# Four-layer graph network: attention masks in pairs, rings in pairs, elu as a maximum

## The chip, the cores and the metric

The kernel runs on one core of a Trainium2 chip. The metric is the device time of one execution in microseconds (us); the median of several runs is given. TensorE multiplies matrices, VectorE and ScalarE work elementwise, GpSimd does small preparation and issues some DMAs, and SyncE issues the others. Each engine works through its own queue in order and waits on semaphores for the others.

## The reference, cut to what matters

Four layers, each with a layer norm, a relu, a graph layer and a residual. The first layer is two graph attentions with 8 heads of 32; the last is one with 4 heads of 64. N is 2500 nodes, E is 40000 edges.

```python
def gat_conv(x, W, al, ar, b, src, dst):          # layer 0, twice
    h = (x @ W).reshape(N, H, D)
    el = jnp.einsum('nhd,hd->nh', h, al)
    er = jnp.einsum('nhd,hd->nh', h, ar)
    e = jax.nn.leaky_relu(el[src] + er[dst], NEG_SLOPE)
    m = jax.ops.segment_max(e, dst, num_segments=N)
    ex = jnp.exp(e - m[dst])
    s = jax.ops.segment_sum(ex, dst, num_segments=N)
    alpha = ex / s[dst]
    out = jax.ops.segment_sum(alpha[:, :, None] * h[src], dst, num_segments=N)
    out = out.reshape(N, H * D) + b
    return jax.nn.elu(out)
...
e = jnp.exp(-jax.nn.leaky_relu(s, ALPHA))          # last layer, each of 4 heads
rowsum = jax.ops.segment_sum(e, src, num_segments=n_nodes)
hp = jax.ops.segment_sum(e[:, None] * h[dst], src, num_segments=n_nodes)
hp = hp / rowsum[:, None]
return jax.nn.elu(hp)                              # and elu again over all heads
```

## The kernel before, in words

The edges are turned once into a dense matrix of counts C, 20 source tiles of 128 rows by 2560 target columns in fp16. `exp(leaky_relu(a + b))` is a product of two exponentials on either side of a + b = 0, so an attention head is a matrix product over masks: where the sum is positive one pair of factors holds, elsewhere the other. The scaled features stand in UV (high and low half in fp16), and TensorE multiplies them by the masked counts.

`attention` runs three times: twice with 8 heads (`split` False) and once with 4 (`split` True). The stage in question is its second half, the loop over heads. A head is cut by target columns into PARTS parts (2 of 1280 columns, or 4 of 640). One part of one head is called a unit here; every attention has 16 units, each over NT = 20 source tiles.

For each tile of a unit:

- ScalarE writes `Rm`, a relu of the target row terms (`rows`, broadcast by a DMA from SyncE, two buffers) with the tile's bias `cB`, scaled so that it is zero or huge (L1109).
- VectorE makes the mask `M` as the minimum of `Rm` and the counts (L1153). With `split` False some tiles are done on VectorE alone in one scalar_tensor_tensor from `rows` (L1156): the last of each four, less the two in MORE_ON_ACT, so 8 of a head's 40.
- In the last attention VectorE also makes `Mn` = C - M, the rest of the counts, for the 12 tiles of a unit that are not in TURNED (L1143). For the 8 in TURNED, TensorE takes five more matmuls with the counts themselves and negated features VS (L1243). With `split` False that is done for every tile (L1248).
- TensorE runs 10 regions (L1240), 132 or 130 columns wide, into four PSUM banks. Two sets of four banks alternate between units.

The rings: `Rm`, `M` and `Mn` have SG slots (4, in the last attention 5). VectorE waits for TensorE to have finished the tile SG before (s_P). ScalarE waits before relu s until mask s - SG is made (`cut`, which in the last attention is the semaphore of `Mn`). TensorE waits for M or for Mn of the tile before its first region.

The evacuation of a unit runs inside the next one. ScalarE, after the relus of the first LEAD tiles (4, in the last attention 7), waits for TensorE's last tile and copies the low sums of four banks to `tl` (L1117, four instructions). VectorE then puts one stage of the rest behind each further mask: `add` (L1180, four instructions), `scale` (L1184, L1185), `both` (L1189), `weight` (L1194), `inverse` (L1198), `mean` (L1202), and `unstash` (L1207). On ScalarE and VectorE head 0 is written out and heads 1 to the last are a loop (`Fori`, L1126 and L1217) with register arithmetic for addresses and waits; TensorE and SyncE are written out.

`elu` works in five batches of four tiles with two buffers `e`. On VectorE `take` makes min(y, 0) (with the bias add before it in the first elu, L1309), ScalarE the exponential (L1350), and VectorE's `finish` max(y, 0) - 1 and then the sum (L1326 or L1329, then L1335). The last elu does two rounds over each batch; the second adds the residual `xr` (L1322, L1333), which a DMA loads at the start of the stage, and the result goes out by DMA per batch. In the first elu, GpSimd loads x again after the third batch's bias add, and the stage ends when both are done.

## Time and profile before

| | |
|---|---|
| median of 3 runs | 2288.17 us (2286.13 to 2288.44) |
| profiled execution, its own time | 2289.7 us |
| its span in the trace | 2287.9 us |
| mean granted TensorE clock | 0.915 of full |
| PE busy | 1750.4 us (77%) |
| PEld busy (weight loads, beside PE) | 1348.8 us (59%) |
| DVE (VectorE) busy | 1639.7 us (72%) |
| ACT (ScalarE) busy | 1398.4 us (61%) |
| POOL (GpSimd) busy | 302.1 us (13%) |

The execution took 1.8 us more than the span that its instructions cover. Busy is the union of the times of an engine's instructions; an instruction starts before the one ahead has ended, so the distance of two starts is shorter than a duration. The share over the whole span is a mean over stages with different limits: the three attentions, the two elu stages, the building of C at the start and the dense layers between are to be read apart.

### The profile page before, as it was taken

The page shows a single profiled execution, that of the slowest core. Times are in us where ns is not written, and L with a number is a line of the kernel's source. Part 1 is how long each engine was busy: PE and PEld are TensorE (multiplying, and loading weights), DVE is VectorE, ACT ScalarE, POOL GpSimd, SP SyncE. Part 2 cuts the span into 40 slices and gives each one's busy share as a digit, 9 for nine tenths or more (in the row PEclk, how much of TensorE's full clock was granted, in tenths as well). Part 3 has the DMA queues.
Part 4 walks back from the last instruction along what each step waited for, and adds up shares of the span by engine and source line. Part 5 has one row for each costly group of instructions (what it writes and reads, how often), then busy time and mean ns, then how long its engine had stood idle before and what let it go on. Part 6 is the DMA issues. An engine that isn't in the chain of part 4 may idle for free. (4 is left out here: it accounts for less than half of the span.)

```text
span 2287.9 us, 64776 instructions
## 1 busy us (share of the span) xinstructions
PE 1750.4 (77%) x21987; PEld 1348.8 (59%) x21987; DVE 1639.7 (72%) x3751; ACT 1398.4 (61%) x2288; POOL 302.1 (13%) x460
## 2 busy tenths in 40 slices
PE   3998874589899639899864299994977984498891
PEld 1333323588888428888863166662537983488881
DVE  6988867899999779999987411113342256899997
ACT  0246774999999569999972321212122354798993
POOL 2465501466100020000000000000000000100000
PEclk9999997799999869999986699997988997699996
DMA  1000001011010001011001200000001010000002
GB/s 61 1 2 2 3 2 34 13 37 37 25 37 25 13 25 37 26 37 37 27 14 50 86 1 0 0 0 6 0 0 41 21 56 22 7 25 20 25 14 91
DMA packets 29718, 54.88 MB, mean 24 GB/s; under 512 B 10222, under 2 KB 20820, under 8 KB 29104
## 3 DMA queue, kind: packets, MB, share of 16 engines
q1 hardware_dynamic: 24608, 43.89, 5.8%
q0 software_dynamic: 4880, 7.80, 1.0%
q8 instruction: 159, 2.61, 0.5%
q14 instruction: 71, 0.58, 0.1%
HBM read 43.19 MB, written 8.49 MB: 23 GB/s over the span
## 5 line engine op out<-in xcount | busy, mean ns | idle before, releaser
L1240 PE MATMUL ps<-R,M 128*128 128x132 f16 (+1 forms) x8640 | 811.2, 222 | 202.4 <-DVE M L1153 102.1
L1109 ACT ACTIVATE Rm<-rows,cB 128x1280 bf16<-128x1280 f32 (+1 forms) x832 | 884.4, 1153 | 22.1 <-DVE Mn L1143 15.7
L1240 PEld LDWEIGHTS ps<-R,M 128*128 128x128 f16 x8640 | 730.6, 97 | 245.2 <-issue 116.2
L1248 PE MATMUL ps<-HB,C 128*128 128x66 f16 x6400 | 596.0, 193 | 0.0
L1153 DVE TENSOR_TENSOR M<-Rm,C 128x1280 f16<-128x1280 bf16 (+1 forms) x832 | 556.2, 693 | 42.6 <-ACT Rm L1109 34.0
L1248 PEld LDWEIGHTS ps<-HB,C 128*128 128x128 f16 x6400 | 571.8, 97 | 0.0
L1512 PE MATMUL psA<-R,C 128*128 128x512 f16 (+1 forms) x1200 | 253.9, 351 | 95.8 <-POOL ones L1564 40.9
L546 DVE TENSOR_SCALAR ohc<-cells,near 128x1280 f16<-128x1280 f16 x387 | 213.8, 553 | 52.6 <-PE acc L571 49.0
L571 PE MATMUL acc<-ohc,ohl 128*128 128x420 f16 (+1 forms) x1161 | 243.7, 348 | 1.7 <-DVE ohl L548 0.3
L1512 PEld LDWEIGHTS psA<-R,C 128*128 (+1 forms) x1200 | 119.3, 100 | 193.0 <-issue 108.5
L1156 DVE SCALAR_TENSOR_TENSOR M<-rows,cN,C 128x1280 f16<-128x1280 f32 x128 | 198.0, 1547 | 0.0
L571 PEld LDWEIGHTS acc<-ohc,ohl 128*128 128x128 f16 x1161 | 89.5, 97 | 148.5 <-DVE ohl L548 95.0
L420 POOL DMA_INDIRECT wd<-wv,wi x104 | 123.0, 1182 | 135.8 <-issue 75.3
L530 ACT ACTIVATE C<-acc 128x420 f16<-128x420 f32 (+1 forms) x120 | 55.7, 542 | 124.7 <-PE acc L571 124.7
L1674 DVE TENSOR_SCALAR rdeg<-psD 128x1 f32 (+1 forms) x20 | 3.2, 159 | 171.7 <-ACT tl L1644 171.7
L548 DVE TENSOR_SCALAR ohl<-lows,bT 128x128 f16<-128x128 f16 x387 | 102.1, 264 | 0.0
L1143 DVE TENSOR_TENSOR Mn<-C,M 128x640 f16<-128x640 f16 x192 | 93.9, 489 | 0.5
L1243 PE MATMUL ps<-VS,C 128*128 128x130 f16 x640 | 89.6, 223 | 0.0
L1240 PE MATMUL ps<-R,Mn 128*128 128x130 f16 x960 | 87.7, 221 | 0.0
L1603 PE MATMUL ps<-xT,W 128*128 128x128 f32 x640 | 76.3, 278 | 1.0 <-ACT xT L1648 1.0
L1652 ACT ACTIVATE hT<-ps,b0c 128x128 f32<-128x128 f32 x80 | 22.9, 368 | 87.0 <-PE ps L1603 87.0
L837 PE MATMUL psH<-Wx,xT 128*128 128x272 f32 (+1 forms) x240 | 70.0, 418 | 7.1 <-ACT xT L799 3.8
(289 smaller groups left out, 2279.9 us busy)
## 6 DMA issues: line engine op xcount, KB each, us to landing
rows<-rowd SPq DMA_DIRECT2D x32, 640.0 KB, 3.9
rows<-rowd SPq DMA_DIRECT2D x16, 320.0 KB, 3.5
xd<-R SPq DMA_DIRECT2D x1, 2560.0 KB, 8.1
xr<-xd SPq DMA_DIRECT2D x20, 128.0 KB, 2.1
xd<-HB SPq DMA_DIRECT2D x1, 2560.0 KB, 9.9
xr<-xd POOLq DMA_DIRECT2D x1, 2560.0 KB, 9.2
R<-in_x SPq DMA_DIRECT2D x1, 2432.0 KB
R<-in_x POOLq DMA_DIRECT2D x1, 2432.0 KB, 10.4
```

The source lines that it names most:

```text
L420: g.indirect_dma_start(out=wd[:, :], out_offset=bass.IndirectOffsetOnAxis(ap=m["wi"][w][:, :], axis=0), in_=m["wv"][w][:, :], in_offset=No ...
L546: v.tensor_scalar(ohc[:, u, :], cells[:, :], near[:, q % 2, ds(k, 1)], None, ALU.is_equal).then_inc(s_oh, 1)
L548: v.tensor_scalar(ohl[:, u, :], lows[:, :], bT[:, ds(k, 1)], None, ALU.is_equal).then_inc(s_oh, 1)
L571: ins = pe.matmul(bank(b, q % 2), ohl[:, u, :], ohc[:, u, d0 * NT:d1 * NT], start=first_, stop=True, skip_group_check=True)
L1109: a.activation(Rm[:, s % SG, :], rows[:, p % 2, :], ACT.Relu, bias=cB[:, ds(h + s * nh, 1)]).then_inc(s_R, 1)
L1143: v.tensor_tensor(Mn[:, u, :], Cs, M[:, u, :], ALU.subtract).then_inc(s_Mn, 1)
L1153: v.tensor_tensor(M[:, u, :], Rm[:, u, :], Cs, ALU.min).then_inc(s_M if s in ONE else s_cut, 1)
L1156: v.scalar_tensor_tensor(M[:, u, :], rows[:, p % 2, :], cN[:, ds(h + s * nh, 1)], Cs, ALU.is_gt, ALU.mult).then_inc(s_M, 1)
L1240: m = pe.matmul(region(p % 2, r), lhsT, rhs, start=first, stop=True, skip_group_check=True)
L1243: m = pe.matmul(region(p % 2, r), C[:, s * NP + p * W + (r % TP) * P:][:, 0:P], VS[:, TURNED.index(s), :, ds(h * cw, cw)], start=False, st ...
L1248: m = pe.matmul(both[:, :, cw:2 * cw], C[:, s * NP + p * W + r * P:][:, 0:P], VP[:, s, :, ds(h * cw, cw)], start=False, stop=True, skip_gr ...
L1512: m = pe.matmul(psA[:, :], lhsT, SPv[:, s, :, :].rearrange("p l c -> p (l c)"), start=s == 0, stop=s == NT - 1)
```

## The change

- **Pairs.** A list of groups takes the place of single tiles. With `split` True a group is two tiles, ten groups a unit. With `split` False five tiles are the groups (0, 1), (2, 3), (4), and in part 0 the last five are (15, 16), (17), (18), (19). One instruction of VectorE makes the mask of a group, of 2560 or of 1280 columns; the rest `Mn` is made a group at a time as well, behind the mask of the next group. The fifth tile of each five, and tile 18 of part 0, are masks on VectorE alone: 9 of a head's 40 tiles.
- **Rings.** `Rm` holds 2 pairs, in the last attention 3. `M` has 5 slots, in the last attention 6. A relu waits for the mask of the group that used its slots. The first relu of a pair waits, the second does not. LEAD is 4, in the last attention 6.
- **TURNED** is now by pairs: tiles 2, 3, 6, 7, 12, 13, 16, 17, again 8.
- **Evacuation.** PSUM is one tile of eight banks. ScalarE's copy is one instruction of 792 or 780 columns, and so is the add; both take 12 regions where 10 are used (two memsets clear the spare ones once). TensorE may start on a set of banks after `add`, where it was after `both`. `q1` is gone: the stages work within `tl`. ScalarE's copy waits for `mean` of the unit before (s_o).
- **Loops.** The loops over heads on ScalarE and VectorE are written out.
- **elu** is max(exp(-relu(-y)) - 1, y). ScalarE makes relu(-y) (`negative`) and the exponential (`power`), one batch ahead; VectorE makes the maximum in one scalar_tensor_tensor, and in the last round the residual add behind it.

The core of the diff (the old code of the elu and TensorE's addresses, whose form alone changes, are left out):

```diff
-MORE_ON_ACT = {(0, 7), (1, 11)}
...
-                TURNED = [t for t in range(NT) if not split or t % 5 in (1, 3)]
+                TURNED = [t for t in range(NT) if not split or t // 2 % 5 in (1, 3)]
...
-                SG = 5 if split else 4
-                LEAD = 7 if split else 4
...
+                SG = 6 if split else 5
+                RP = 3 if split else 2
+                LEAD = 6 if split else 4
...
+                    if split:
+                        return [(s, s + 1) for s in range(0, NT, 2)]
+                    some = [g for s in range(0, NT, 5) for g in ((s, s + 1), (s + 2, s + 3), (s + 4,))]
+                    return some if p else some[:-2] + [(NT - 3,), (NT - 2,), (NT - 1,)]
+                by_vector = lambda p, s: not split and (s % 5 == 4 or p == 0 and s == NT - 2)
+                units = [(q, q // PARTS, q % PARTS) for q in range(nh * PARTS)]
...
-                    Rm = ph.sb("Rm", [P, SG, W], bf16)
+                    Rm = ph.sb("Rm", [P, 2 * RP, W], bf16)
...
-                    ps = [[ph.ps(f"ps{b}{j}", [P, 3 * 2 * XW]) for j in range(NB)] for b in range(2)]
...
+                    ps = ph.ps("ps", [P, 2, NB, 512])
...
-                                if s in on_act[p]:
-                                    cut(a, h * PARTS + p, s - SG, hold)
-                                    a.activation(Rm[:, s % SG, :], rows[:, p % 2, :], ACT.Relu,
-                                                 bias=cB[:, ds(h + s * nh, 1)]).then_inc(s_R, 1)
...
-                            q = h * PARTS + p
-                            hold(a, s_P, (q + 1) * NT + SG)
-                            hold(a, s_E, q + 2)
...
+                        def relus(q, h, p, s0, s1):
+                            a.wait_ge(s_row[q % 2], (q // 2 + 1) * 16)
+                            for g in groups_of(p):
+                                n = index[q, g]
+                                if not s0 <= g[0] < s1 or n not in relu_of:
+                                    continue
+                                k = relu_of[n]
+                                if k >= RP:
+                                    a.wait_ge(s_M, relu_groups[k - RP] + 1)
+                                for w, s in enumerate(g):
+                                    a.activation(Rm[:, k % RP * 2 + w, :], rows[:, q % 2, :], ACT.Relu,
+                                                 bias=cB[:, h + s * nh:h + s * nh + 1]).then_inc(s_R, 1)
...
+                        def evacuate(q):
+                            a.wait_ge(s_P, (q + 1) * NT)
+                            a.wait_ge(s_o, q)
+                            a.activation(tl_banks, sums(q % 2, 1), ACT.Copy, scale=1 / LO).then_inc(s_tl, 1)
...
+                        for q, h, p in units:
+                            relus(q, h, p, 0, LEAD)
+                            if q:
+                                evacuate(q - 1)
+                            relus(q, h, p, LEAD, NT)
+                        evacuate(len(units) - 1)
...
-                            v.wait_ge(s_cut, (h * PARTS + p) * len(TWO) + TWO.index(s) + 1)
-                            Cs = C[:, s * NP + p * W:s * NP + (p + 1) * W]
-                            v.tensor_tensor(Mn[:, u, :], Cs, M[:, u, :], ALU.subtract).then_inc(s_Mn, 1)
...
-                                    v.tensor_tensor(M[:, u, :], Rm[:, u, :], Cs, ALU.min).then_inc(s_M if s in ONE else s_cut, 1)
-                                else:
...
+                            v.memset(ps[:, b, NB - 1, 2 * XW:6 * XW], 0.0).then_inc(s_E, 1)
...
+                            n, last = index[q, g], q * NT + g[-1]
+                            if last >= SG:
+                                v.wait_ge(s_P, last - SG + 1)
+                            dest = M[:, slot(q, g[0]):slot(q, g[0]) + len(g), :]
+                            part = Cv[:, g[0]:g[0] + len(g), p * W:(p + 1) * W]
+                            if n in relu_of:
+                                k = relu_of[n] % RP * 2
+                                v.wait_ge(s_R, relus_to[n])
+                                v.tensor_tensor(dest, Rm[:, k:k + len(g), :], part, ALU.min).then_inc(s_M, 1)
...
+                                s = g[0]
+                                v.wait_ge(s_row[q % 2], (q // 2 + 1) * 16)
+                                v.scalar_tensor_tensor(dest[:, 0, :], rows[:, q % 2, :], cN[:, h + s * nh:h + s * nh + 1],
+                                                       part[:, 0, :], ALU.is_gt, ALU.mult).then_inc(s_M, 1)
...
+                            n = index[q, g]
+                            if n in twice_to:
+                                v.wait_ge(s_M, n + 1)
+                                u = slice(slot(q, g[0]), slot(q, g[0]) + 2)
+                                v.tensor_tensor(Mn[:, u, :], Cv[:, g[0]:g[0] + 2, p * W:(p + 1) * W], M[:, u, :],
+                                                ALU.subtract).then_inc(s_Mn, 1)
...
-                                hold(v, s_tl, q + 1)
-                                for r, n, part in banks(p % 2, 0):
-                                    ch(v.tensor_tensor(tl[:, r:r + n, :], part, tl[:, r:r + n, :], ALU.add))
+                                v.wait_ge(s_tl, q + 1)
+                                v.tensor_tensor(tl_banks, sums(q % 2, 0), tl_banks, ALU.add).then_inc(s_E, 1)
...
+                        for q, h, p in units:
+                            masks(q, h, p, [g for g in groups_of(p) if g[0] < LEAD])
+                            masks(q, h, p, [g for g in groups_of(p) if g[0] >= LEAD], evacuation(*units[q - 1]) if q else ())
...
+                                n = index[q, g]
+                                if n in twice_to:
+                                    pe.wait_ge(s_Mn, twice_to[n])
+                                else:
+                                    pe.wait_ge(s_M, n + 1)
...
+                    def finish(n):
+                        i, w = order[n]
+                        more = residual is not None and w == rounds - 1
+                        v.wait_ge(s_ee, n + 1)
+                        if raw(w):
+                            for j in range(TB):
+                                ins = v.scalar_tensor_tensor(by_head(y(i))[:, j], by_head(wide(e[:, n % 2, :]))[:, j], -1.0,
+                                                             heads_of(i)[:, j], ALU.add, ALU.max)
+                            ins.then_inc(s_o, 1)
+                        elif more:
+                            v.scalar_tensor_tensor(y(i), wide(e[:, n % 2, :]), -1.0, y(i), ALU.add, ALU.max).then_inc(s_v, 1)
+                            v.wait_ge(s_v, i + 1)
+                            v.wait_ge(residual[1], 16)
+                            v.tensor_tensor(y(i), y(i), wide(residual[0][:, i * BW:(i + 1) * BW]), ALU.add).then_inc(s_o, 1)
+                        else:
+                            v.scalar_tensor_tensor(y(i), wide(e[:, n % 2, :]), -1.0, y(i), ALU.add, ALU.max).then_inc(s_o, 1)
...
+                    def negative(n):
                         i, w = order[n]
                         if n >= 2:
-                            v.wait_ge(s_o, n - 1)
-                        if w == 0 and bias_dram is None:
+                            a.wait_ge(s_o, n - 1)
...
+                                ins = a.activation(by_head(wide(e[:, n % 2, :]))[:, j], heads_of(i)[:, j], ACT.Relu, scale=-1.0)
...
                         if w == 0:
...
+                            a.wait_ge(s_in, (i + 1) * TB)
                         else:
-                            v.wait_ge(s_o, order.index((i, 0)) + 1)
-                        v.tensor_scalar(wide(e[:, n % 2, :]), y(i), 0.0, None, ALU.min).then_inc(s_e, 1)
...
                         a.wait_ge(s_e, n + 1)
-                        a.activation(e[:, n % 2, :], e[:, n % 2, :], ACT.Exp).then_inc(s_ee, 1)
+                        a.activation(e[:, n % 2, :], e[:, n % 2, :], ACT.Exp, scale=-1.0).then_inc(s_ee, 1)
...
+                    negative(0)
+                    negative(1)
+                    power(0)
+                    for n in range(1, len(order)):
+                        power(n)
+                        if n + 1 < len(order):
+                            negative(n + 1)
```

VectorE in the last attention, where the evacuation of a unit stands between masks, before. Behind each name is the source; x2 is two in a row.

```order
L1153 TENSOR_TENSOR M<-Rm,C 128x640
L1180 TENSOR_TENSOR tl<-ps_510,tl 128x195
L1180 TENSOR_TENSOR tl<-ps_511,tl 128x195
L1180 TENSOR_TENSOR tl<-ps_512,tl 128x195
L1180 TENSOR_TENSOR tl<-ps_513,tl 128x65
L1153 TENSOR_TENSOR M<-Rm,C 128x640
L1143 TENSOR_TENSOR Mn<-C,M 128x640
L1184 TENSOR_TENSOR tl<-tl,F_469 128x325
L1185 TENSOR_TENSOR q_508<-tl,F_468 128x325
L1153 TENSOR_TENSOR M<-Rm,C 128x640
L1189 TENSOR_TENSOR q_508<-q_508,tl 128x325
L1153 TENSOR_TENSOR M<-Rm,C 128x640
```

And after, the same place, with L1140 the mask, L1152 the rest and L1180 the add:

```order
L1152 TENSOR_TENSOR Mn<-C,M 128x1280
L1180 TENSOR_TENSOR tl<-ps,tl 128x780
L1140 TENSOR_TENSOR M<-Rm,C 128x1280
L1184 TENSOR_TENSOR tl<-tl,F_453 128x325
L1185 TENSOR_TENSOR tl<-tl,F_452 128x325
L1140 TENSOR_TENSOR M<-Rm,C 128x1280
L1152 TENSOR_TENSOR Mn<-C,M 128x1280
L1189 TENSOR_TENSOR tl<-tl 128x325
L1140 TENSOR_TENSOR M<-Rm,C 128x1280
L1152 TENSOR_TENSOR Mn<-C,M 128x1280
L1193 TENSOR_SCALAR rec<-tl 128x5
```

Where a row held one tile's mask or rest it now holds those of two tiles, so each stage of the evacuation stands behind a mask of two tiles; the add is one instruction.

On ScalarE the first evacuation of the last attention stands behind 26 relus, where it stood behind 27.

VectorE at the end of the last elu, before: the second round of the third batch, then the fourth and the last batch:

```order
L1322 SCALAR_TENSOR_TENSOR R<-R,xr 128x1024
L1333 SCALAR_TENSOR_TENSOR R<-e,R 128x1024
L1304 TENSOR_SCALAR e<-HB 128x256 x4
L1322 SCALAR_TENSOR_TENSOR R<-R,xr 128x1024
L1333 SCALAR_TENSOR_TENSOR R<-e,R 128x1024
L1326 TENSOR_SCALAR R<-HB 128x256 x4
L1335 TENSOR_TENSOR R<-R,e 128x1024
L1314 TENSOR_SCALAR e<-R 128x1024
L1322 SCALAR_TENSOR_TENSOR R<-R,xr 128x1024
L1333 SCALAR_TENSOR_TENSOR R<-e,R 128x1024
```

And after, with L1303 and L1307 the maximum and L1310 the residual:

```order
L1307 SCALAR_TENSOR_TENSOR R<-e,R 128x1024
L1310 TENSOR_TENSOR R<-R,xr 128x1024
L1307 SCALAR_TENSOR_TENSOR R<-e,R 128x1024
L1310 TENSOR_TENSOR R<-R,xr 128x1024
L1303 SCALAR_TENSOR_TENSOR R<-e,HB 128x256 x4
L1307 SCALAR_TENSOR_TENSOR R<-e,R 128x1024
L1310 TENSOR_TENSOR R<-R,xr 128x1024
```

The minimum has left VectorE, and the maximum and the sum have become one instruction; the residual add stands behind each second maximum.

## Rows read from the trace of the kernel before

**Rows 1.** windows by stage: us, busy PE, PEld, DVE, ACT, POOL, PEclk, DMA share, GB/s

```profile
847.00:1191.00 344.00, 304.27 (x6400) 288.26 (x6400) 333.02 (x488) 335.46 (x320) 0.00 (x0) 0.99 0.09 29
...
1972.00:2246.00 274.00, 238.38 (x3840) 227.65 (x3840) 254.09 (x672) 248.12 (x384) 0.00 (x0) 0.97 0.07 19
2246.00:2288.00 42.00, 0.00 (x0) 0.00 (x0) 30.68 (x60) 10.46 (x10) 5.25 (x7) 0.50 0.31 124
```

**Rows 2.** groups by shape, whole trace: count | busy us, mean duration ns | idle before

```profile
L1109 ACT ACTIVATE Rm<-rows,cB 128x1280 bf16<-128x1280 f32 x512 | 646.9, 1361 | 2.7 <-DVEq L1132 2.2
L1153 DVE TENSOR_TENSOR M<-Rm,C 128x1280 f16<-128x1280 bf16 x512 | 406.3, 821 | 21.3 <-ACT Rm L1109 19.4
...
L1109 ACT ACTIVATE Rm<-rows,cB 128x640 bf16<-128x640 f32 x320 | 237.5, 820 | 19.4 <-DVE Mn L1143 15.7 <-DVEq L1134 1.2
```

**Rows 3.** the timeline, ScalarE, second attention: start us, us, line, count

```profile
933.63 0.91 ACT L1117 ACTIVATE tl<-ps 128x198 f32<-128x198 f32 x4
934.40 20.16 ACT L1109 ACTIVATE Rm<-rows,cB 128x1280 bf16<-128x1280 f32 x16
...
975.70 0.56 ACT L1117 ACTIVATE tl<-ps 128x198 f32<-128x198 f32 x2
```

**Rows 4.** the timeline, VectorE, second attention

```profile
930.70 1.55 DVE L1156 SCALAR_TENSOR_TENSOR M<-rows,cN,C 128x1280 f16<-128x1280 f32 x1
932.16 2.50 DVE L1153 TENSOR_TENSOR M<-Rm,C 128x1280 f16<-128x1280 bf16 x3
...
945.85 2.29 DVE L1153 TENSOR_TENSOR M<-Rm,C 128x1280 f16<-128x1280 bf16 x3
948.05 1.55 DVE L1156 SCALAR_TENSOR_TENSOR M<-rows,cN,C 128x1280 f16<-128x1280 f32 x1
...
957.63 1.03 DVE L1180 TENSOR_TENSOR tl<-ps,tl 128x198 f32<-128x198 f32 x4
958.58 0.81 DVE L1153 TENSOR_TENSOR M<-Rm,C 128x1280 f16<-128x1280 bf16 x1
```

**Rows 5.** the timeline, ScalarE, last attention

```profile
2024.19 0.85 ACT L1117 ACTIVATE tl<-ps 128x195 f32<-128x195 f32 x4
2024.94 5.15 ACT L1109 ACTIVATE Rm<-rows,cB 128x640 bf16<-128x640 f32 x7
...
2040.34 0.85 ACT L1117 ACTIVATE tl<-ps 128x195 f32<-128x195 f32 x4
...
2226.25 0.85 ACT L1117 ACTIVATE tl<-ps 128x195 f32<-128x195 f32 x4
...
2241.06 0.90 ACT L1117 ACTIVATE tl<-ps 128x195 f32<-128x195 f32 x4 [3.52 <-PE ps L1240]
```

**Rows 6.** the timeline, VectorE, last attention, about two back edges of the loop

```profile
2105.01 0.89 DVE L1153 TENSOR_TENSOR M<-Rm,C 128x640 f16<-128x640 bf16 x2 [2.84 <-ACT Rm L1109]
2105.82 0.48 DVE L1143 TENSOR_TENSOR Mn<-C,M 128x640 f16<-128x640 f16 x1
...
2173.43 0.89 DVE L1153 TENSOR_TENSOR M<-Rm,C 128x640 f16<-128x640 bf16 x2 [3.14 <-issue]
```

**Rows 7.** the timeline, TensorE, last attention

```profile
2025.87 0.45 PE L1240 MATMUL ps<-R,M 128*128 128x130 f16 x5
2026.15 0.45 PE L1240 MATMUL ps<-R,Mn 128*128 128x130 f16 x5
```

**Rows 8.** the timeline of the first elu and of the last

```profile
1203.72 1.79 POOL L158 DMA_DIRECT2D R<-in_x  x1 [0.31 <-POOL R L1359]
...
1214.84 1.22 DVE L1335 TENSOR_TENSOR HB<-HB,e 128x1024 f32<-128x1024 f32 x1
...
2257.20 1.23 DVE L1322 SCALAR_TENSOR_TENSOR R<-R,xr 128x1024 f32<-128x1024 f32 x1 [2.18 <-DMA xr<-xd]
...
2279.44 1.06 ACT L1350 ACTIVATE e<-e 128x1024 f32<-128x1024 f32 x1 [4.34 <-DVE e L1314]
...
2280.78 1.23 DVE L1333 SCALAR_TENSOR_TENSOR R<-e,R 128x1024 f32<-128x1024 f32 x1
```

251 lines of the change are left out of this document (93 added, 158 removed).

## The prediction, made before the changed kernel ran

> **What bounds the kernel now.** I read the windows by stage first. The second attention takes 344 us, the first is its twin, the last takes 274: some 960 of 2288 us, and VectorE and ScalarE are both busy over 90% of it [rows 1]. TensorE is not far behind but waits for masks. The change touches these stages and the two elu stages and nothing else, so the sum is over these.
>
> Then the shapes and the timelines, for the start-to-start distance ("pitch") of each instruction, which is shorter than its duration [rows 2]. ScalarE: sixteen relus of 1280 columns run from 934.40 to 954.60, 1.26 each, a few of them held by a wait; 1.253 is the undisturbed pitch. Its evacuation before them has 0.77 [rows 3]. VectorE: a mask of 1280 columns has a pitch of 0.735 (three from 945.85 to 948.05), the one-instruction mask from rows (L1156) 1.46, the four adds of an evacuation 0.95 [rows 4]; a mask or a second part of 640 columns 0.40 (two from 2105.01 to 2105.82) [rows 6].
>
> One head of the first two attentions costs ScalarE 32 x 1.253 + 2 x 0.77 = 41.6, and VectorE 32 x 0.735 + 8 x 1.46 = 35.2 of masks plus 5.5 of evacuation plus 0.24 of copy = 41.0. The measured head is 975.70 - 933.63 = 42.07 [rows 3]. **Both engines are full**; ScalarE is 0.5 ahead. In the last attention a unit (20 tiles) costs VectorE 20 x 0.40 + 12 x 0.40 + 0.93 + 1.8 = about 15.5 (1.8 for the stages behind the adds), ScalarE 20 x 0.72 + 0.74 = 15.1 (seven relus in 5.15, the last one lasting 0.82), and takes 2040.34 - 2024.19 = 16.15; over the stage I use 16.24 [rows 5].
>
> **First and second attention (16 heads).** Removed: one relu in 32 on ScalarE, 1.253 a head. Moved: that mask goes to VectorE, +1.46 - 0.735. Merged: of 31 masks 30 go in pairs. A pair of 2560 columns is not in the trace; 640 and 1280 columns have 0.40 and 0.735, so a fixed part of 0.067 and 0.522 a thousand columns, and a pair costs 1.40, saving 0.07. The upper bound is two single ones (1.47); the lower is streaming alone (1.34). The four adds become one of 792 columns over whole banks, two regions of them padding: 0.89 for 0.95. The evacuation on ScalarE likewise pays for the padding: 0.71 for 0.77. So ScalarE: 31 x 1.253 + 1.4 = 40.3. VectorE: 15 x 1.40 + 0.735 + 9 x 1.46 + 5.4 + 0.24 = 40.55. If nothing waited, a head would fall from 42.07 to 40.6.
>
> But a pair of masks starts only when its second relu is done, and the ring Rm holds two pairs, so a relu waits for a whole pair of masks. I walked both queues through a head. From the end of mask (10,11) ScalarE runs eight relus without a break up to tile 3 of the next unit: 7 x 1.253 + 1.37 + 0.07 for two wake-ups = 10.2. VectorE has only masks (12,13), 14, (15,16), (17,18), 19, (0,1) and two stages for that: 3 x 1.40 + 2 x 1.46 + 1.40 + 0.5 = 9.0. It waits 0.5 at (17,18) and 0.75 at (2,3); the other part of the head adds 0.23. That is 1.5 of waits: 40.55 + 1.5 = **42.05 a head, against 42.07**. The saving is given back. The pair's bounds move this by +1.0 and -1.0 with part of it hidden, so -0.7 to +0.9 a head. Each stage also starts later, as the first mask needs two relus: +0.4 twice. Sum for 16 heads: +1 (-10 to +14).
>
> The Trainium skill, in VectorE: DVE Perf Modes, section The DRAIN you can't avoid, says that the next instruction does not start until the pipe is empty, and advises to minimise the count of instructions. By its breakdown (about 150 cycles of decode in each) a merged pair would save about 0.16, not 0.07, an estimate. The rows speak against it: durations of 0.82 [rows 2] stand at pitches of 0.735 [rows 4], so part of the fixed cost is overlapped already. By the page a head would be some 1.4 us shorter on VectorE; that is the first rival below.
>
> **Last attention (16 units).** Work: VectorE 10 masks and 6 second parts of 1280 columns at 0.735, one add 0.88, stages 1.8 = 14.4 for 15.5. ScalarE stays at 15.1. But here waits form a chain. Relus 6 and 7 of a unit stand behind the evacuation of the unit before (LEAD is 6 where it was 7), and the evacuation waits for TensorE's last tile. Link by link, from the start of mask (6,7):
> - VectorE to the end of the second part of (14,15): six masks 4.41, four second parts 2.94, add 0.88, scale 0.82, sum 0.41, weight and inverse 0.18, and 0.67 of waiting, since mask (16,17) needs the ring of six slots freed by TensorE's pair (10,11), itself behind the second part of (10,11). Together 10.3, and 0.1 to its end.
> - TensorE cannot start pair (14,15) earlier. It then has 20 + 30 + 20 matmuls at 0.0577 [rows 7] = 4.04, and 0.2 to start and end.
> - ScalarE: 0.13 to wake, evacuation 0.70, relu 0.72, relu 0.82 to its end: 2.4. Then mask (6,7) of the next unit may start.
>
> Sum 17.05 a unit, above the engines' 14.4, 15.1 and 13.9. Against 16.24: +0.8, times 14 = +11.3. The last unit, where ScalarE had no relus to do and took 14.8 [rows 5], follows the same chain: +2.2. The start: +0.5. Bounds: with the add at 0.95 or the pair at 0.70 or 0.765 the chain is 16.8 to 17.3.
>
> The loops over heads are written out, which removes the stalls at VectorE's back edge: it idles 2.84 and 3.14 there [rows 6], with the masks after them late too; the two heads concerned are 3.2 and 4.0 longer than four undisturbed units. That is -7.2. In the other two attentions the back edge (here at 930.6, ahead of the mask at 930.70) shows no idle time [rows 4], so nothing goes. Written out code is fetched in a straight line, as TensorE's already is; I count nothing for it. Sum of the stage: 11.3 + 2.2 + 0.5 - 7.2 = **+6.8** (-1 to +12).
>
> **The elu stages.** Two VectorE passes and a final sum become one pass (e - 1 max y); the minimum becomes a relu on ScalarE. In the last one ScalarE works 10.5 of 42 us [rows 1], so it has room. The Trainium skill, in ScalarE: Activation LUTs, section Rules for kernel authors, puts relu, max and min on VectorE. Here the rows say that VectorE is the one that is full, so I go against it.
>
> The stage still waits for xr until 2257.20 and then ran to 2282.01 [rows 8], 24.8 us. After it, by the new order: finish of the waiting batch 1.2; the next (pass and residual) to 3.7; its successors wait for relu, exp on ScalarE (four relus of 256 to 1.3, exp 1.06 [rows 8]): batches end at 5.2, 7.7, 10.7, 13.1; the fifth group has only one batch, so its relu, exp, pass, relu, exp, pass, residual stand in a row: 13.2, 14.6, 16.8, 19.3. That is -5.5 (-3 to -7). The first elu is bound by the load of x from 1203.72, landing about 1215.6, beside VectorE's end at 1216.06 [rows 8]. The third bias add that starts it stands where it stood: VectorE's end goes to 1211, and 0.5 is gained.
>
> **Sum.** +1 + 6.8 - 6.0 = +1.8 on the profiled execution of 2289.7 us, so 2291.5. That execution is 1.5 above the median of the runs shown, so the median comes to **2290.0**. This kernel's measurement can tell about 0.2% (4.6 us) from no change.
>
> **The rivals.**
> - **A, the pairs are cheaper and flow better** than walked: VectorE pairs nearer 1.34, and the waits of 1.5 a head mostly absorbed. A head at 41.2 gives -14, the last attention at 16.6 a unit gives 0: together about 2270. For it: the engines' own work allows 40.6 and 15.1. Against it: the same walk through the code before gives 41.9 and 16.25 a head and unit, where the trace has 42.07 and 16.24.
> - **B, slower: the chain through the evacuation is longer**, place as above, price 16 x 0.4 or more. It decides when TensorE falls out of step: by the walk it waits 3.2 us a unit for second parts, at most 1.0 at a time. The granted clock of this stage is 0.97 as it is, where the second attention has 0.99 [rows 1]. If the clock fell at times in the last attention, 70 matmuls cost up to 4 us more in such a unit; four such units give +16, with a head at 42.4 another +5: about 2308.
> - **C, the attention stages barely move and only the elu and the back edge pay**: -13 with the last attention at 16.3 a unit: about 2277.
>
> **How the numbers follow.** Forecast case (within 2284 to 2297) 0.5, A 0.13, C 0.15, B 0.22. Two in ten are left out of 2277 to 2303. Chances: the forecast case gives 0.39 same, 0.09 slower, 0.02 faster; A adds 0.13 to faster, C 0.13 to faster and 0.02 to same, B 0.22 to slower: faster 0.28, same 0.41, slower 0.31.
>
> **What would show it.** Right: in the last attention a unit of about 17.0 between evacuations, ScalarE idle about 1.8 before each for TensorE, VectorE idle about 1.2 at mask (6,7) for a relu, and no idle of 3 at a back edge. In the first two a head of about 42.0 with VectorE waiting for relus at (17,18) and (2,3), the pair at a pitch of 1.40. The last elu 5 to 6 us shorter. Wrong: a pitch of the pair off 1.40 by over 0.05, a unit under 16.6, or a granted clock below 0.9 in a unit.

## The result, and the profile after

The changed kernel takes 2295.45 us (median of 8 runs, 2293.17 to 2297.58) where the kernel before takes 2286.98 (8 runs beside them, 2286.13 to 2288.91). The ratio is 1.0035, with an interval of 1.0024 to 1.0045: **slower by 8 us**. The profiled span is 2295.8 us for 2287.9, so the trace holds 7.9 of it.

The windows of the second and of the last attention, after, as long as those of [rows 1] and with the same columns; the windows stand 1 and 6 us later, as the stages start 1.7 and 6.3 us later.

```profile
848.00:1192.00 344.00, 303.91 (x6400) 289.00 (x6400) 325.93 (x317) 324.97 (x264) 0.00 (x0) 0.99 0.09 29
1978.00:2252.00 274.00, 233.04 (x3795) 221.15 (x3796) 234.60 (x363) 244.45 (x335) 0.00 (x0) 0.98 0.07 19
```

Against [rows 1] VectorE and ScalarE have 7 and 10 us less busy time in the second attention, yet the stage isn't shorter. In the last, VectorE has 19 us less, and 274 us hold 3795 matmuls where they held 3840. **Work went and idle time came.** The timelines say where. ScalarE in the second attention, after (start us, us, line, count, and in brackets the idle time before it with what ended it):

```profile
936.54 0.81 ACT L1116 ACTIVATE tl<-ps 128x792 f32<-128x792 f32 x1
...
947.60 3.87 ACT L1110 ACTIVATE Rm<-rows,cB 128x1280 bf16<-128x1280 f32 x3 [0.23 <-DVE M L1140]
952.64 5.12 ACT L1110 ACTIVATE Rm<-rows,cB 128x1280 bf16<-128x1280 f32 x4 [1.17 <-DVE M L1140]
...
968.73 10.13 ACT L1110 ACTIVATE Rm<-rows,cB 128x1280 bf16<-128x1280 f32 x8 [0.23 <-DVE M L1140]
978.77 0.81 ACT L1116 ACTIVATE tl<-ps 128x792 f32<-128x792 f32 x1
```

A head is 978.77 - 936.54 = 42.23 us, for 42.07 [rows 3]. ScalarE, which ran 16 relus in one piece in [rows 3], now stops three times a head for a mask of a pair (0.23 in each part, and 1.17). VectorE at the same place:

```profile
931.72 1.49 DVE L1140 TENSOR_TENSOR M<-Rm,C 128x2560 f16<-128x2560 bf16 x1 [0.52 <-ACT Rm L1110]
...
936.74 1.49 DVE L1140 TENSOR_TENSOR M<-Rm,C 128x2560 f16<-128x2560 bf16 x1 [0.66 <-ACT Rm L1110]
...
939.61 0.98 DVE L1180 TENSOR_TENSOR tl<-ps,tl 128x792 f32<-128x792 f32 x1
940.50 1.49 DVE L1140 TENSOR_TENSOR M<-Rm,C 128x2560 f16<-128x2560 bf16 x1
941.90 0.50 DVE L1184 TENSOR_TENSOR tl<-tl,F 128x330 f32<-128x330 f32 x1
...
957.86 1.49 DVE L1140 TENSOR_TENSOR M<-Rm,C 128x2560 f16<-128x2560 bf16 x1 [0.26 <-ACT Rm L1110]
```

The pair has a pitch of 941.90 - 940.50 = 1.40, the add of 940.50 - 939.61 = 0.89, both as costed. The waits for a second relu are 0.52 at (17,18), 0.66 at (2,3) and 0.26 in the other part: 1.44 a head. Last attention, ScalarE and then VectorE:

```profile
2051.13 0.82 ACT L1116 ACTIVATE tl<-ps 128x780 f32<-128x780 f32 x1 [1.58 <-PE ps L1233]
...
2068.11 0.82 ACT L1116 ACTIVATE tl<-ps 128x780 f32<-128x780 f32 x1 [1.58 <-PE ps L1233]
```

```profile
2053.49 0.82 DVE L1140 TENSOR_TENSOR M<-Rm,C 128x1280 f16<-128x1280 bf16 x1 [1.21 <-ACT Rm L1110]
...
2062.24 0.83 DVE L1140 TENSOR_TENSOR M<-Rm,C 128x1280 f16<-128x1280 bf16 x1 [0.51 <-PE ps L1233]
...
2066.95 0.83 DVE L1140 TENSOR_TENSOR M<-Rm,C 128x1280 f16<-128x1280 bf16 x1 [0.41 <-PE ps L1236]
```

A unit is 16.97 or 16.98, the same 15 times over, where the undisturbed ones took 16.14 to 16.3 [rows 5]. Each has ScalarE's 1.58 before the evacuation and VectorE's 1.21 at mask (6,7); the idle 3 us of [rows 6] are gone. At the end of the two elu stages:

```profile
1213.31 1.22 DVE L1312 SCALAR_TENSOR_TENSOR HB<-e,HB 128x1024 f32<-128x1024 f32 x1 [1.14 <-ACT e L1341]
1219.42 0.37 SPq L1381 DMA_DIRECT2D Wl<-wd  x1
```

```profile
2254.81 0.82 ACT L1116 ACTIVATE tl<-ps 128x780 f32<-128x780 f32 x1 [6.08 <-PE ps L1233]
...
2288.60 1.23 DVE L1310 TENSOR_TENSOR R<-R,xr 128x1024 f32<-128x1024 f32 x1
```

VectorE ends the first elu at 1214.53, and the next stage starts at 1219.42, 4.9 later: not VectorE but the load of x bounds it. From the last evacuation to the end of the span it is 41.0 us, where it was 46.8 (2241.06 [rows 5] to 2287.9), and VectorE's last instruction ends 35.0 after that evacuation for 41.0 before (2282.01 [rows 8]).

**Where the 7.9 us are**, cut at the starts of the first relu of each attention, before:

```profile
418.93 2.61 ACT L1109 ACTIVATE Rm<-rows,cB 128x1280 bf16<-128x1280 f32 x2 [1.11 <-DVEq L1132]
846.67 2.62 ACT L1109 ACTIVATE Rm<-rows,cB 128x1280 bf16<-128x1280 f32 x2 [1.12 <-DVEq L1132]
...
1972.09 8.74 ACT L1109 ACTIVATE Rm<-rows,cB 128x640 bf16<-128x640 f32 x12 [1.19 <-DVEq L1134]
```

and after:

```profile
419.72 2.61 ACT L1110 ACTIVATE Rm<-rows,cB 128x1280 bf16<-128x1280 f32 x2 [0.95 <-PEq L100]
848.38 2.61 ACT L1110 ACTIVATE Rm<-rows,cB 128x1280 bf16<-128x1280 f32 x2 [0.96 <-PEq L100]
...
1978.40 2.98 ACT L1110 ACTIVATE Rm<-rows,cB 128x640 bf16<-128x640 f32 x4 [0.96 <-PEq L100]
```

| stretch (same cuts in both traces) | before | after | difference | in the sum of the prediction |
|---|---|---|---|---|
| up to the first attention's relus | 418.9 | 419.7 | +0.8 | 0 |
| first attention to its last evacuation | 340.0 | 341.4 | +1.4 | +0.5 |
| from there to the second attention | 87.8 | 87.3 | -0.5 | 0 |
| second attention | 339.3 | 341.1 | +1.8 | +0.5 |
| from there through the first elu to the next matmul | 48.0 | 46.9 | -1.1 | -0.5 |
| the stages between, untouched | 738.1 | 742.0 | +3.9 | 0 |
| last attention: to its first evacuation | 19.8 | 21.8 | +2.0 | +0.5 |
| last attention: 15 units | 249.2 | 254.6 | +5.4 | +6.3 |
| last evacuation to the end | 46.8 | 41.0 | -5.9 | -5.5 |

The touched stages came out at +3.1 where the sum had +1.8. The rest of the 7.9, some 4.7 us, lies in the first stretch and in the stages between, whose code nobody changed.

### The profile page after: what moved, and what is told of

Same layout as the page of the kernel before. It is cut to its first block and busy times, and to the rows that moved or that the text cites. A ratio compares the mean times of both kernels' runs of the same rounds, so it can differ in the third digit from the quotient of the medians.

```text
span 2295.8 us, 60157 instructions
## 1 busy us (share of the span) xinstructions
PE 1749.4 (76%) x21987; PEld 1348.2 (59%) x21987; DVE 1594.0 (69%) x3077; ACT 1389.6 (61%) x2158; POOL 330.1 (14%) x460
## 5 line engine op out<-in xcount | busy, mean ns | idle before, releaser
L1110 ACT ACTIVATE Rm<-rows,cB 128x1280 bf16<-128x1280 f32 (+1 forms) x816 | 863.6, 1141 | 29.9 <-DVE M L1140 26.0
L1140 DVE TENSOR_TENSOR M<-Rm,C 128x2560 f16<-128x2560 bf16 (+1 forms) x416 | 498.3, 1201 | 69.1 <-ACT Rm L1110 48.6
L1144 DVE SCALAR_TENSOR_TENSOR M<-rows,cN,C 128x1280 f16<-128x1280 f32 x144 | 221.4, 1547 | 0.0
L419 POOL DMA_INDIRECT wd<-wv,wi x104 | 132.8, 1277 | 128.5 <-issue 64.8
L1152 DVE TENSOR_TENSOR Mn<-C,M 128x1280 f16<-128x1280 f16 x96 | 78.7, 820 | 0.5
```

Source lines behind the costliest of these rows:

```text
L419: g.indirect_dma_start(out=wd[:, :], out_offset=bass.IndirectOffsetOnAxis(ap=m["wi"][w][:, :], axis=0), in_=m["wv"][w][:, :], in_offset=No ...
L1110: a.activation(Rm[:, k % RP * 2 + w, :], rows[:, q % 2, :], ACT.Relu, bias=cB[:, h + s * nh:h + s * nh + 1]).then_inc(s_R, 1)
L1140: v.tensor_tensor(dest, Rm[:, k:k + len(g), :], part, ALU.min).then_inc(s_M, 1)
L1144: v.scalar_tensor_tensor(dest[:, 0, :], rows[:, q % 2, :], cN[:, h + s * nh:h + s * nh + 1], part[:, 0, :], ALU.is_gt, ALU.mult).then_inc( ...
L1152: v.tensor_tensor(Mn[:, u, :], Cv[:, g[0]:g[0] + 2, p * W:(p + 1) * W], M[:, u, :], ALU.subtract).then_inc(s_Mn, 1)
```

## The experiments

Eleven kernels in three groups; each group shares the runs of the kernel before on its chip. "Unit" is the time between two evacuations of ScalarE in the last attention, "head" that of two in the first two. The changed kernel ran beside other runs of the kernel before; the medians of that kernel are 2286.98, 2288.13, 2287.14 and 2286.40 us, so a difference to the changed kernel can be off by about 1 us.

**One part alone: the elu.** The code of `elu` of the changed kernel in the kernel before, all of it and nothing else:

```diff
-                        v.tensor_scalar(wide(e[:, n % 2, :]), y(i), 0.0, None, ALU.min).then_inc(s_e, 1)
+                        a.activation(wide(e[:, n % 2, :]), y(i), ACT.Relu, scale=-1.0).then_inc(s_e, 1)
...
+                            v.scalar_tensor_tensor(y(i), wide(e[:, n % 2, :]), -1.0, y(i), ALU.add, ALU.max).then_inc(s_o, 1)
```

> The kernel before with the elu of the changed one and nothing else. Theory (the two elu stages pay what the sum said, and lengthen nothing): the last elu 5.5 us shorter, the first 0.5 to 1, so about 2280.5. Rival (the relus on ScalarE and the wait for xr cost more than the minimum on VectorE): within 2 us of before. The stages between the second and the last attention are untouched here as in the changed kernel, where they took 3.9 us more: if that comes with the elu code it is seen here (2284), if it comes with the written-out attention loops it is not.

2283.7 us, ratio 0.9978 (0.9968 to 0.9988). From the last evacuation to the end it takes 41.2 us for 46.8, -5.6, and up to the matmul after the first elu -1.2. Both terms hold. But the whole is 4.4 us below the kernel before in its group (2288.13), 2 short of the theory. The untouched stages took 739.3 for 738.1; whether that is a part of the 3.9 one execution doesn't tell, and it is taken up below.

**One part alone: the loops.** Written out in the kernel before:

```diff
-                        with a.Fori(1, nh) as h:
-                            body(h, False)
+                        for h in range(1, nh):
+                            body(h, False)
...
-                        with v.Fori(1, nh) as h:
-                            ch.begin(h - 1, PARTS * (NB + 5) + (0 if split else 1))
-                            body(h, False)
-                            ch.end(nh - 1)
+                        for h in range(1, nh):
+                            body(h, False)
```

> The kernel before with the two loops over heads written out on ScalarE and VectorE, all else as it was. Theory: the idle times of about 3 us at two back edges of the last attention go, with the masks that they made late, -7 us, nothing in the first two: about 2280, with every unit of the last attention at 16.2. Rival (longer code costs elsewhere): the same 7 us won there, and 4 us lost in the untouched stages between the second and the last attention, where small loops of VectorE run: 2284.

2276.82 us, ratio 0.9947 (0.9931 to 0.9964): 11 us less than the 2288.13 of its group, and not 7. The last attention gave 8.5 of its 249.2 us back, every unit at 16.14. The others came in the first two attentions, where nothing had been expected. ScalarE there:

```profile
930.60 0.88 ACT L1117 ACTIVATE tl<-ps 128x198 f32<-128x198 f32 x4
931.35 20.16 ACT L1109 ACTIVATE Rm<-rows,cB 128x1280 bf16<-128x1280 f32 x16
...
972.35 0.88 ACT L1117 ACTIVATE tl<-ps 128x198 f32<-128x198 f32 x4
```

A head is 41.75 us for 42.07. A relu starts 1.25 us after the one ahead. Between 910 and 1160 us of the kernel before, the evacuation starts 1.38 us or more after the relu ahead of it in all twelve units, and 6 of 190 relus are 0.14 us late, 0.44 us a head together; in loops_out the evacuation comes after 1.25 to 1.30 us and 6 of 192 relus are 0.07 us late, 0.13 a head. That is the difference. In the loop the values of these waits are worked out in registers. The run takes the loop and the registers away together, so it doesn't show which of the two costs the time. The rival lost: the untouched stages took 738.4 us, as before.

**The last attention: the place of the evacuation.**

```diff
-                LEAD = 6 if split else 4
+                LEAD = 8 if split else 4
```

> The changed kernel with the evacuation of the last attention behind the relus of 8 tiles where it stood behind 6. Theory (the unit is bound by the chain that runs through the evacuation, the relus 6 and 7 behind it and the pair of masks (6,7)): those relus are ahead of the evacuation, the 1.21 us wait of VectorE at mask (6,7) goes, and a unit takes 16.3 for 16.97: 11 us less, about 2285. Rival (the six slots of M bind, with the waits for TensorE of 0.51 and 0.42): the wait only moves to another mask and a unit stays above 16.8: 2293 or more. Rival 2: the stages begin one mask later and run past the end of the unit: slower than the changed kernel.

2285.24 us, ratio 0.9986 (0.9977 to 0.9996), 10 us less than the changed kernel. ScalarE:

```profile
2046.43 0.80 ACT L1116 ACTIVATE tl<-ps 128x780 f32<-128x780 f32 x1
...
2062.81 0.80 ACT L1116 ACTIVATE tl<-ps 128x780 f32<-128x780 f32 x1
```

A unit is 16.38 (16.3 expected), with no wait before the evacuation. The chain through it was what bound the unit. Now VectorE waits for slots of M (0.76, 0.28, 0.20 and 0.17 us for TensorE in one unit, 1.4 in all, where it was 0.93), and ScalarE for masks, so the first rival has its part, but behind the chain.

**The last attention with single tiles.**

```diff
-                TURNED = [t for t in range(NT) if not split or t // 2 % 5 in (1, 3)]
+                TURNED = [t for t in range(NT) if not split or t % 5 in (1, 3)]
...
-                SG = 6 if split else 5
-                RP = 3 if split else 2
-                LEAD = 6 if split else 4
+                SG = 5
+                RP = 5 if split else 2
+                GW = 1 if split else 2
+                LEAD = 7 if split else 4
...
-                        return [(s, s + 1) for s in range(0, NT, 2)]
+                        return [(s,) for s in range(NT)]
...
-                    Rm = ph.sb("Rm", [P, 2 * RP, W], bf16)
+                    Rm = ph.sb("Rm", [P, GW * RP, W], bf16)
```

> The changed kernel with single tiles in the last attention: masks and rests of 640 columns, five slots, LEAD 7 and the tiles of TURNED as before; the one-instruction evacuation, the written-out loops and everything in the first two attentions stay. Theory (the pairs make the chain long, since each step waits for two tiles): VectorE's work rises by 1.0 us a unit and the unit still falls, from 16.97 to about 15.7 (20 relus 14.4, copy 0.70, one wait): 20 us less, about 2275. Rival (the evacuation in one instruction or its wait for the mean stage is what made the unit long): a unit stays above 16.8.

2269.39 us, ratio 0.9916 (0.9899 to 0.9932), 26 us less than the changed kernel.

```profile
2041.70 0.80 ACT L1117 ACTIVATE tl<-ps 128x780 f32<-128x780 f32 x1
2042.40 15.02 ACT L1111 ACTIVATE Rm<-rows,cB 128x640 bf16<-128x640 f32 x20
2057.32 0.80 ACT L1117 ACTIVATE tl<-ps 128x780 f32<-128x780 f32 x1
```

A unit is 15.62, though VectorE has more instructions in it. VectorE is now what bounds it: over five such units it is busy 77.96 of 78.13 us. The unit is also 0.5 less than the 16.14 with written-out loops alone, though both use single tiles. Two things differ: the one-instruction evacuation, and what a relu waits for. So the relu's wait was put back:

```diff
-                                    a.wait_ge(s_M, relu_groups[k - RP] + 1)
+                                    n0 = relu_groups[k - RP]
+                                    if n0 in twice_to:
+                                        a.wait_ge(s_Mn, twice_to[n0])
+                                    else:
+                                        a.wait_ge(s_M, n0 + 1)
```

> The kernel single_last, with each relu of the last attention waiting for the rest Mn of the tile that used its slot, where there is one, as the kernel before did, and not for its mask alone. It asks why a unit took 15.63 us there and 16.14 with the loops alone written out. Theory (ScalarE was held by the wait for Mn, one tile later than needed): a unit goes back to about 16.1. Rival (the one-instruction evacuation, and TensorE's banks being free after the add, gave the 0.5): it stays at 15.6.

2275.94 us, ratio 0.9955 (0.9938 to 0.9971).

```profile
2047.89 9.85 ACT L1115 ACTIVATE Rm<-rows,cB 128x640 bf16<-128x640 f32 x13 [0.42 <-DVE Mn L1157]
```

The unit is 16.01, with ScalarE's 0.42 us for Mn behind the evacuation in every one. Of the 0.5, 0.4 is this wait; all the rest, the one-instruction evacuation included, is 0.1. The rest Mn is made from M and C, so in the kernel before this wait held back a slot of Rm that nobody read any more.

**The last attention with pairs and room.** LEAD 8 as above, eight slots of M, and a ring Mn of its own, since it holds only the twelve tiles that need one:

```diff
-                SG = 6 if split else 5
+                SG = 8 if split else 5
...
-                    Mn = ph.sb("Mn", [P, SG, W], f16) if split else None
+                    Mn = ph.sb("Mn", [P, 6, W], f16) if split else None
...
-                                v.tensor_tensor(Mn[:, u, :], Cv[:, g[0]:g[0] + 2, p * W:(p + 1) * W], M[:, u, :],
+                                un = (twice_to[n] - 1) % 3 * 2
+                                v.tensor_tensor(Mn[:, un:un + 2, :], Cv[:, g[0]:g[0] + 2, p * W:(p + 1) * W], M[:, u, :],
```

> The changed kernel with its pairs, and in the last attention LEAD 8, a ring M of eight slots and a ring Mn of six slots of its own. Theory (pairs are slow there by too small rings and the place of the evacuation, not by themselves): with the relus 6 and 7 ahead of the evacuation and no mask waiting for TensorE, ScalarE bounds the unit by its 20 relus and the copy, 15.1 for 16.97 us: 28 us less than the changed kernel, about 2267, and less than with single tiles (15.63). Rival (the pair's wait for its second relu is a cost of its own whatever the rings): a unit stays at 15.7 or above.

2265.82 us, ratio 0.9908 (0.9891 to 0.9924).

```profile
2039.68 0.81 ACT L1116 ACTIVATE tl<-ps 128x780 f32<-128x780 f32 x1
2040.38 14.50 ACT L1110 ACTIVATE Rm<-rows,cB 128x640 bf16<-128x640 f32 x20
2054.77 0.81 ACT L1116 ACTIVATE tl<-ps 128x780 f32<-128x780 f32 x1
```

A unit is 15.09: twenty relus and the copy, with nothing between. This is the rival's defeat: **pairs are not slow here by themselves**. With room they beat single tiles by 0.5 a unit; in the change as it was made they lose 1.35 to them. The single tiles had five slots and LEAD 7, but more room could not have helped them: VectorE had no idle time there, while over five units of these pairs it is busy 72.54 of 75.48 us and ScalarE all the time. Pairs win because VectorE has about 1 us less to do in a unit. Eight slots with LEAD 6 were not tried, so what the slots give (16.38 to 15.09) is shown for LEAD 8 only.

**The first two attentions with single tiles.**

```diff
-                by_vector = lambda p, s: not split and (s % 5 == 4 or p == 0 and s == NT - 2)
+                by_vector = lambda p, s: not split and (s % 4 == 3 and (p, s) not in ((0, 7), (1, 11)))
...
-                    some = [g for s in range(0, NT, 5) for g in ((s, s + 1), (s + 2, s + 3), (s + 4,))]
-                    return some if p else some[:-2] + [(NT - 3,), (NT - 2,), (NT - 1,)]
+                    return [(s,) for s in range(NT)]
```

> The changed kernel with single tiles in the first two attentions (32 masks and 8 one-instruction masks a head as before, four slots of Rm and of M); the one-instruction evacuation and the written-out loops stay, the last attention keeps its pairs. Theory (a pair waits for its second relu, and the ring of two pairs holds ScalarE back by 1.4 us a head): without pairs ScalarE runs through, a head is its 32 relus and 2 copies, 41.5 for 42.2 us: 11 us less than the changed kernel, about 2284. Rival (each merged instruction pays more than its waits cost, so the pairs help): a head at 42.2 or above: 2295 or more.

2280.16 us, ratio 0.9967 (0.9955 to 0.9978), 15 us less than the changed kernel.

```profile
929.60 0.83 ACT L1116 ACTIVATE tl<-ps 128x792 f32<-128x792 f32 x1
930.31 20.17 ACT L1110 ACTIVATE Rm<-rows,cB 128x1280 bf16<-128x1280 f32 x16
...
971.12 0.84 ACT L1116 ACTIVATE tl<-ps 128x792 f32<-128x792 f32 x1
```

A head is 41.52, to the hundredth the 32 relus and two copies of the theory. Pairs cost 0.7 a head here. Fifteen and not eleven were gained. From their first relus to their last evacuations the two attentions take 12.0 us less, 1.8 of it in the two first units; the untouched stages take 737.3 us for 742.0, and 1.1 is lost ahead of the first attention. Whether pairs with a third pair of Rm would win here was not tried.

**One mask a head more on VectorE,** undone:

```diff
-                    return some if p else some[:-2] + [(NT - 3,), (NT - 2,), (NT - 1,)]
+                    return some
...
-                by_vector = lambda p, s: not split and (s % 5 == 4 or p == 0 and s == NT - 2)
+                by_vector = lambda p, s: not split and s % 5 == 4
```

> The changed kernel with 32 relus and 8 one-instruction masks a head in the first two attentions, where it has 31 and 9: all tiles in fives of two pairs and one alone. Theory (ScalarE isn't the bound there any more, but stands in waits of 1.4 us a head for pairs of masks): the relu that comes back fills a wait, and a head stays at 42.1 to 42.2, within 3 us of the changed kernel. Rival (the relu moved to VectorE did shorten ScalarE's path): 1.25 a head more, 20 us, about 2315.

2293.69 us, ratio 1.0028 (1.0019 to 1.0038), within 2 us of the changed kernel.

```profile
948.09 10.15 ACT L1110 ACTIVATE Rm<-rows,cB 128x1280 bf16<-128x1280 f32 x8 [0.22 <-DVE M L1140]
```

The 1.17 us for a mask are gone, filled by the relu that came back, and the head stays at 42.23 (937.04 to 979.25 is 42.21). VectorE's waits for relus grow from 1.4 to 2.2 us a head instead. Taking a relu off ScalarE bought nothing.

**The parts together.** Single tiles everywhere:

> The changed kernel with single tiles in all three attentions; what stays of the change is the one-instruction evacuation, the written-out loops and the elu. Theory: the two parts add, 41.5 a head and 15.6 a unit: about 2259, 28 us below the kernel before. Rival (both were freed by the same thing, so that they overlap): above 2265.

2258.03 us, ratio 0.9869 (0.9853 to 0.9886); head 41.5, unit 15.63. This is the change without its pairs and their rings: it is 29 us faster than the kernel before, and the pairs as they were made cost 37. And single tiles in the first two with roomy pairs in the last (the edits of single_first and of pairs_roomy):

> The changed kernel with single tiles in the first two attentions and, in the last, the pairs with eight slots of M, six of Mn and LEAD 8. Theory: the two gains add, 41.5 a head and 15.1 a unit: about 2256. Rival: the unit of the last attention isn't shorter than with single tiles, 2262 or more.

2252.19 us, ratio 0.9849 (0.9833 to 0.9866): **35 us faster than the kernel before and 43 than the changed one**. The parts add: 15 and 30 taken alone, 43 together.

**The untouched stages.** There are small loops of VectorE among them. One splits an operand into two parts; it runs at three places, five passes at each. VectorE at the first of them, before, and after:

```profile
1287.96 1.14 DVE L1490 TENSOR_SCALAR L<-HB,lsc 128x256 f32 x4 [0.25 <-DVE R L1495]
...
1291.31 1.14 DVE L1490 TENSOR_SCALAR L<-HB,lsc 128x256 f32 x4 [0.25 <-DVE R L1495]
```

```profile
1291.77 1.25 DVE L1489 TENSOR_SCALAR L<-HB,lsc 128x256 f32 x4 [0.34 <-DVE R L1494]
...
1295.31 1.25 DVE L1489 TENSOR_SCALAR L<-HB,lsc 128x256 f32 x4 [0.30 <-DVE R L1494]
```

The same instructions take 3.35 us a pass before and 3.53 after. elu_only has 3.52 as well, loops_out 3.36. At the middle place nothing like it is seen: 3.35 before, 3.38 after. The new elu has 15 instructions less on VectorE ahead of the loop (319 where there were 334, counted in the traces from the last evacuation of the second attention), so the loop's code stands elsewhere. The next kernel is elu_only with the count restored:

```diff
+                    if bias_dram is not None:
+                        for _ in range(15):
+                            v.sem_inc(dum, 1)
```

> The kernel before with the new elu (as in elu_only), and 15 semaphore increments that nobody waits for on VectorE at the end of the first elu. The new elu has 15 instructions less on VectorE up to there, so these put every later instruction of VectorE back to the place that it has in the kernel before. Theory (the untouched loop that splits the operand into two parts, five passes of 3.35 us before and of 3.52 in elu_only, depends on where its instructions stand): the passes take 3.36 again, at both places where the loop runs, and the kernel is about 2 us faster than elu_only. Rival (something else of the new elu, such as ScalarE's code or data left in a buffer, slows the loop): the passes stay at 3.52.

2280.0 us, ratio 0.9973 (0.9962 to 0.9983).

```profile
1284.51 1.14 DVE L1499 TENSOR_SCALAR L<-HB,lsc 128x256 f32 x4 [0.62 <-DVEq L1494]
...
1287.88 1.14 DVE L1499 TENSOR_SCALAR L<-HB,lsc 128x256 f32 x4 [0.26 <-DVE R L1504]
```

The passes take 3.37 again, and at the last place 3.23 (3.22 before, 3.46 after). **How many instructions stand ahead of a loop changes its time.** Whether it is the place of the code or something else that moves with the count isn't shown. The ratios of the two kernels to the kernel before differ in the right way, but by less than their intervals tell; the verdict rests on the rows. They fit the other kernels: lead8, single_last, pairs_roomy and wait_rest, which differ from the changed kernel only behind these loops, have its 3.52, and those that differ from it ahead of them have 3.38. Over all thirteen traces, with the untouched stages cut at the same two instructions:

| passes at the first place | kernels | untouched stages, us | mean |
|---|---|---|---|
| 3.35 to 3.38 | before, loops_out, single_first, single_all, best, first_32_8, elu_pad | 734.5 to 738.4 | 737.1 |
| 3.51 to 3.53 | after, elu_only, lead8, single_last, pairs_roomy, wait_rest | 738.1 to 742.0 | 739.4 |

That is 2.3 us of the 3.9. The loops themselves account for it: at the first place four passes take 14.4 for 13.4 us, at the last 14.2 for 12.9. The other 1.6, and the 0.8 ahead of the first attention, are no more than the scatter of one execution: within each row of the table the stages differ by 4 us, and the first attention starts anywhere from 418.4 to 420.9.

## Why the prediction was right, and where not

The time is inside the range, and the named chain and waits were found, but the predicted 2290.0 is 5.5 us under the measured time. The sum said +1.8 us, less than the 4.6 us (0.2%) that it called the least to be told from no change; the kernel is slower by 8.5 us, or 0.35%. Of the 6 us between them in the trace (+7.9 for +1.8), 4.7 lie in stages that the sum didn't hold and 1.3 in those that it did. That these 1.3 are so few is in part luck, since terms off both ways stand behind them.

- **The pair's pitch, the add, the copy** (1.40, 0.89, 0.71): measured to 0.01. The estimate of 0.16 saved a pair, from the 150 cycles of decode that the Trainium skill gives in VectorE: DVE Perf Modes, section Side-by-side: where the cycles go for N=2048 bf16, didn't come true; a pair saves 0.07. The section that the prediction names, The DRAIN you can't avoid, itself adds that an instruction that is not held starts earlier, and the rows agree: masks of 1.49 stand at a pitch of 1.40. (The advice on the count of instructions stands in another section, Rules for kernel authors.) Rival A's cheaper pair is out.
- **First two attentions.** The waits for second relus were put at 0.5, 0.75 and 0.23 a head; they are 0.52, 0.66 and 0.26. The head is 42.23 for the 42.05 of the walk. The two attentions together are 3.2 us longer for the +1 of the sum: their first units cost 0.9 each for 0.4, and the heads behind them give the other 1.4. **A step failed without being seen in the sum**: that the back edge in these attentions "shows no idle time [rows 4], so nothing goes". Written-out loops alone bring 0.32 a head (loops_out), so against that kernel the pairs cost 0.48 a head, and against single tiles with the one-instruction evacuation 0.7 (single_first). The saving was given back, as said, and more had been saved than said.
- **The last attention.** The chain was right link by link: unit 17.05 predicted, 16.97 measured; ScalarE idle 1.8 predicted, 1.58; VectorE idle 1.2 predicted, 1.21. lead8 cut it and the unit fell to 16.38. The part of the chain that waits for slots was put at 0.67 and is 0.51. The mis-sized term is the start, +0.5 where it measured +2.0. TensorE's first matmul, before and after:

```profile
1974.71 0.70 PE L1240 MATMUL ps<-R,M 128*128 128x130 f16 x5 [39.41 <-DVE Mn L1143]
...
1983.12 0.70 PE L1233 MATMUL ps<-R,M 128*128 128x130 f16 x5 [40.67 <-DVE Mn L1152]
```

  It waits for the rest Mn of the first group. With single tiles that is 2.62 us behind the stage's first relu, with pairs, where four relus and two masks of two tiles stand ahead of that rest, 4.72. From the first matmul to the first evacuation it is 17.1 us for 17.2, so the later matmul is the whole +2.0. TensorE comes out of idle time at a granted clock of 0.50, the lower of its two levels (1.2 GHz), and is given 1.00 later, when it is at work. The windows of the first unit, before and after:

```profile
1975.00:1978.00 3.00, 3.00 (x30) 3.00 (x29) 2.51 (x6) 3.00 (x6) 0.00 (x0) 0.50 0.00 0
1978.00:1981.00 3.00, 3.00 (x43) 3.00 (x41) 1.99 (x6) 2.83 (x4) 0.00 (x0) 0.75 0.02 5
```

```profile
1984.00:1987.00 3.00, 3.00 (x31) 3.00 (x29) 1.51 (x2) 3.00 (x5) 0.00 (x0) 0.50 0.00 0
1987.00:1990.00 3.00, 3.00 (x46) 3.00 (x45) 1.24 (x3) 2.23 (x4) 0.00 (x0) 0.83 0.02 5
```

  It works at 0.50 for 4.8 us before and for 4.9 after, so the clock takes the same from both and isn't the reason. It does move the first unit from one execution to the next: with 3.9, 4.8 and 5.8 us at 0.50 (loops_out, before, elu_only) the first evacuation comes after 19.45, 19.82 and 20.29 us, and with 4.0, 4.9 and 5.4 us (single_first, after, first_32_8) after 21.41, 21.81 and 22.05.
- **The back edges.** -7.2 predicted; loops_out brought -8.5 in the stage, 7.2 of it in the four units about the two back edges and most of the rest in units at 16.14 for 16.24. The prediction took the whole 7.2 for stalls. In the kernel before the granted clock also falls to 0.50 at both back edges and nowhere else behind the first unit; stretches with the first, with none and with the second:

```profile
2080.00:2120.00 40.00, 34.54 (x551) 32.95 (x551) 35.99 (x97) 35.35 (x55) 0.00 (x0) 0.96 0.07 19
2120.00:2160.00 40.00, 36.61 (x613) 35.12 (x611) 38.56 (x103) 38.48 (x62) 0.00 (x0) 1.00 0.10 27
2160.00:2200.00 40.00, 33.80 (x514) 32.25 (x511) 35.27 (x94) 34.31 (x53) 0.00 (x0) 0.91 0.06 19
```

  TensorE had been idle there for 2.72 and 3.02 us. The units at the two places take 18.84 and 19.14, and the next ones 16.82 and 17.39 for 16.24. In loops_out, which has no such idle time, the clock stays at 1.00 behind the first unit. What share of the 7.2 is the low clock isn't shown.
- **The elu.** -5.5 and -0.5 predicted, -5.9 and -1.1 measured, -5.6 and -1.2 in elu_only. In the first elu the load of x is issued 17.3 us after the last evacuation for 17.7 and the stage ends 12.7 us behind the issue for 13.3; over all kernels with the new elu this stretch is 46.6 to 47.8 us for 48.0, so the gain there is anything from 0.2 to 1.5. Putting a relu on ScalarE, against the rule of the Trainium skill (ScalarE: Activation LUTs, section Rules for kernel authors), was right for this stage, where VectorE was busy 30.7 of 42 us and ScalarE 10.5 [rows 1]: elu_only is 0.2% faster. That run also merges VectorE's passes; the two were not tried apart.
- **The untouched stages** were counted at nothing: "The change touches these stages and the two elu stages and nothing else". That is the largest step that failed: +4.7 us in the traces for 0, of which 2.3 come with the count of instructions ahead of a loop at two of its places, and the rest is within the scatter.

Rival C (only elu and back edge pay) is out by the units. Of rival B the direction came true without its mechanism: no unit of the last attention was longer than 16.98, and behind the first the clock stayed at 1.00.

## What to carry to other kernels

Merging two steps of a pipeline saves the fixed cost of one instruction (0.07 us here) and doubles what each neighbour waits for; whether it pays is decided by the rings and by what stands between, not by the instruction. Before a merge, walk the queues from the evacuation on, give the rings room for what is now in flight and put the evacuation behind whatever the next step needs: the same pairs were 1.35 us a unit slower than single tiles as first made, 0.75 slower with the evacuation moved, and 0.5 faster with eight slots for six as well. And look at what each wait is for: a relu that waited for the rest Mn, which doesn't read its buffer, cost 0.4 us in each unit. A change of several parts is best measured part by part: here 29 us of gain stood beside 37 of loss.
